# A residual layer with a conditioned linear part, in fp32: the order of the loads, the place of the bias, and the last group by rows

## The reference

```python
hidden = concat([cond, cond], axis=-1)                      # (4, 512)
x_mean = mean(x, axis=1, keepdims=True)
fused = concat([x, x_mean * ones, hidden[:, None] * ones], axis=-1)   # (4, 1024, 1536)
out = x + relu(einsum('bld,do->blo', fused, W) + b)
```

## Time and profile before

| | |
|---|---|
| median of 3 runs | 119.73 us (119.43 to 119.76) |
| profiled execution, first to last instruction | span 117.4 us |
| profiled execution, its own time | not listed apart from the three runs |
| TensorE busy | 103.1 us, 88% of the span |
| VectorE / ACT / POOL busy | 87.0 / 48.2 / 46.7 us |
| moved by DMA | 20.28 MB, mean 173 GB/s |

### The profile page before, as it was taken

How to read it: one execution, slowest core, us unless ns; L and a number is a source line. 1 busy time by engine, 2 the same in 40 slices (tenths; PEclk the granted TensorE clock), 3 DMA queues, 4 the chain that set the end, 5 groups by cost and what they waited for, 6 DMA issues and landing times.

```text
span 117.4 us, 1775 instructions
## 1 busy us (share of the span) xinstructions
PE 103.1 (88%) x490; PEld 82.0 (70%) x490; DVE 87.0 (74%) x163; ACT 48.2 (41%) x118; POOL 46.7 (40%) x46
## 2 busy tenths in 40 slices
PE   5919999935999879997999999999999999999910
PEld 2309998812478568875888888778888886999900
DVE  1028859860289799999999995499999996897640
ACT  4057516700105988006848700077495001833310
POOL 6358310034000000089785840046856339992000
PEclk9995999999599999999999999999999999999995
DMA  2999999999999999990785809400076292295986
GB/s 89 258 228 229 220 212 232 380 240 223 222 224 221 224 220 221 220 167 4 163 197 127 236 12 233 113 0 0 0 170 188 51 248 58 62 241 135 253 219 170
DMA packets 35975, 20.28 MB, mean 173 GB/s; under 512 B 1920, under 2 KB 34688, under 8 KB 35968
## 3 DMA queue, kind: packets, MB, share of 16 engines
q1 hardware_dynamic: 34528, 18.88, 74.5%
q10 hardware_dynamic: 1248, 0.79, 2.5%
q0 software_dynamic: 192, 0.52, 1.8%
HBM read 11.80 MB, written 8.39 MB: 172 GB/s over the span
## 4 chain that ended last, share of the span: by engine, by line
PE 49%; SPq 23%; DMA 10%; DVE 9%; issue 3%; ACT 2%; ACTq 0%
PE ps_y L410 47%; SPq L162 15%; DMA xa<-in_x_dram 10%; SPq L141 3%; DVE back L317 2%; SPq L171 2%; DVE w2x L334 2%; DVE ps_xt L300 2%; PE ps_mean L428 1%; ACT xh L236 1%; DVE xl L306 1%; ACT relu_t L256 1%; DVE bias_row L348 1%; SPq L169 1%; SPq L173 1%
## 5 line engine op out<-in xcount | busy, mean ns | idle before, releaser
L410 PE MATMUL ps_y<-xh,w1h 128*128 128x256 f32 (+2 forms) x160 | 55.1, 370 | 4.3 <-ACT xh L236 2.4
L206 POOL TENSOR_TENSOR xa<-xa,back 128x512 f32 x28 | 36.0, 1304 | 42.8 <-DVE back L317 42.8
L410 PE MATMUL ps_y<-xl,w1h 128*128 128x256 f32 (+2 forms) x160 | 52.3, 353 | 0.0
L410 PE MATMUL ps_y<-xh,w1l 128*128 (+2 forms) x144 | 50.3, 366 | 0.0
L410 PEld LDWEIGHTS ps_y<-xh,w1h 128*128 128x128 f32 x160 | 29.5, 197 | 11.0 <-issue 4.4
L256 ACT ACTIVATE relu_t<-ps_y,bias 128x512 f32<-128x512 f32 (+1 forms) x32 | 19.9, 633 | 33.0 <-DVE bias L351 25.6
L410 PEld LDWEIGHTS ps_y<-xl,w1h 128*128 128x128 f32 x160 | 29.5, 196 | 4.8 <-issue 1.2
L300 DVE STREAM_TRANSPOSE ps_xt<-xa 128x512 f32<-128x512 f32 (+1 forms) x36 | 22.2, 641 | 13.5 <-DMA xa<-in_x_dram 13.2
L236 ACT ACTIVATE xh<-ps_xt 128x512 fp32r<-128x512 f32 (+1 forms) x36 | 19.7, 549 | 26.2 <-DVE ps_xt L300 25.9
L410 PEld LDWEIGHTS ps_y<-xh,w1l 128*128 128x128 f32 x144 | 27.1, 189 | 4.5
L306 DVE TENSOR_TENSOR xl<-ps_xt,xh 128x512 fp32r<-128x512 f32 (+1 forms) x36 | 22.2, 618 | 4.2 <-ACT xh L236 4.2
(11 more groups left out here) (21 smaller groups left out, 22.1 us busy)
## 6 DMA issues: line engine op xcount, KB each, us to landing
xa<-in_x_dram SPq DMA_DIRECT2D x28, 256.0 KB, 6.5
out_dram<-xa SPq DMA_DIRECT2D x28, 256.0 KB, 3.8
xa<-in_x_dram SPq DMA_DIRECT2D x8, 128.0 KB, 5.9
w<-in_L_cond_W_dram SPq DMA_DIRECT2D x4, 256.0 KB, 6.8
w<-in_L_cond_W_dram SPq DMA_DIRECT2D x2, 512.0 KB, 9.7
w<-in_L_cond_W_dram POOLq DMA_DIRECT2D x4, 128.0 KB, 4.7
out_dram<-xa SPq DMA_DIRECT2D x4, 128.0 KB, 2.7
out_dram<-xa ACTq DMA_DIRECT2D x4, 128.0 KB, 2.4
```

The costliest lines, as they stand in the source:

```text
L206: nc.gpsimd.tensor_tensor(rows, rows, back[:, t], ALU.add).then_inc(added, 1)
L410: return nc.tensor.matmul(ps_y[:, t, ls], lhs, rhs, start=start, stop=stop, skip_group_check=True)
```

## The change

W1 is loaded by blocks k of 128 features (four DMAs of 64 KB each), behind x0's first half, which comes on two queues. W1's block 0 is rounded half on VectorE and half on ACT; block 1 on ACT in two halves that PE takes as pairs of tiles. PE does group 0's low-W1 products between the others and takes the first two tiles of group 1 block by block. All eight tiles of batch 0 and two of group 2 are set aside by ACT (`save`; two of them in `w1`'s place). W3, its halves not summed, is multiplied inside group 2's second tile, 16 instructions of 128 columns to four quadrants; the mean products are four such instructions each. The last group is computed by rows (x stationary, W1 moving), its bias comes as a line through DRAM, x is read again by rows, and it is stored by rows. Two adds of group 6 move from POOL to VectorE. Warm-up products are 12.

```diff
-WARM = 14
+WARM = 12
+    DVE_ADDS = 2
+    SAVED = H * NK + 2
+    bias_line = nc.dram_tensor("bias_line", [D], F32).ap()
...
 sync:
-            load_x0(sp, 0)
-            load_w1(sp, 1, range(0, 2), w1_landed)
-            load_x0(sp, 1)
-            load_x(1, 1)
...
+            load_x0(sp, 0, LOW)
+            load_w1(sp, 0, 1, LOW)
+            load_w1(sp, 1, 2, LOW)
+            load_w1(sp, 2, 3, LOW)
+            load_w1(sp, 3, 4, LOW)
+            load_x0(sp, 1, ORDER)
+            load_x(sp, 1, ORDER)
+            load_x(sp, 2, ORDER)
+            load_w2(sp, ORDER)
+            load_x(sp, 3, ORDER)
             for r in range(2):
                 sp.dma_start(w3[:, r], w3v[r]).then_inc(w3_landed, 16)
+            for g in range(SLOTS, G):
+                load_x(sp, g, ORDER)
+            sp.wait_ge(const_summed, 1)
+            for r in range(NR):
+                sp.dma_start(last_x[:, r], x_rows[LAST, :, r]).then_inc(last_x_landed, 16)
+            for g in range(LAST):
+                if g == LAST - 2:
+                    sp.wait_ge(bias_summed, B)
+                    for j in range(NQ):
+                        sp.dma_start(bias_line[P * j:P * j + P], bias_row[Q * j + B - 1]).then_inc(bias_stored, 16)
+                    sp.wait_ge(bias_stored, 16 * NQ)
+                    sp.dma_start(last_bias[:], bias_line.partition_broadcast(P)).then_inc(last_bias_landed, 16)
...
 gpsimd:
+            pool.wait_ge(x0_landed[0], 16 * NQ)
+            for j in HIGH:
+                pool.dma_start(w1[Q * j:Q * j + Q, NK - 1:NK], wv[0, j, :, NK - 1:NK]).then_inc(w1_rest_landed, 16)
...
-            nc.gpsimd.tensor_tensor(w3sum[:], w3[:, 0], w3[:, 1], ALU.add).then_inc(w3_added, 1)
...
 scalar:
+            load_x0(act, 0, HIGH)
             act.wait_ge(ones_set, 1)
             nc.scalar.activation(act_warm[:], ones[:, 0:1], ACT.Relu)
+            load_w1(act, 0, 1, HIGH)
+            load_w1(act, 1, 2, HIGH)
+            load_w1(act, 2, 3, HIGH)
...
             x_high(0)
+            w1_high(0, DVE_T, NK)
             x_high(1)
+            w1_high(1, 0, NK // 2)
+            w1_high(1, NK // 2, NK)
             for k in range(2, NK):
+                x_high(k)
                 w1_high(k)
...
 vector:
             turn_x(0)
+            turn_x(1)
+            dve.wait_ge(w1_landed[0], 16 * NQ)
+            nc.vector.tensor_copy(as_tiles(w1h[:, 0])[:, 0:DVE_T], by_tile(w1[:, 0])[:, 0:DVE_T]).then_inc(w1h_first_ready, 1)
+            x_low(0)
...
+            def last_rows(step, r, y, cols):
+                biased = relu_t[:, NK + r, cols]
+                dve.wait_ge(y_ready, NK * LAST + step)
+                nc.vector.tensor_tensor(biased, y, last_bias[:, cols], ALU.add).then_inc(last_biased, 1)
+                dve.wait_ge(last_biased, step)
+                nc.vector.scalar_tensor_tensor(out=last_x[:, r, cols], in0=biased, scalar=0.0, in1=last_x[:, r, cols],
+                                               op0=ALU.max, op1=ALU.add).then_inc(last_added, 1)
...
 tensor:
-                nc.tensor.matmul(ps_mean[:], ones[:], w2x[:], start=True, stop=True).then_inc(mean_done, 1)
+                for j in range(NQ):
+                    last = nc.tensor.matmul(ps_mean[Q * j:Q * j + Q, 0:P], ones[:, 0:Q], w2x[:, P * j:P * j + P], start=True, stop=True)
+                last.then_inc(mean_done, 1)
...
+            def const_product():
+                pe.wait_ge(cond_spread, 1)
+                pe.wait_ge(w3_landed, 16 * 2)
+                for r in range(2):
+                    for k in range(CK):
+                        for j in range(NQ):
+                            last = nc.tensor.matmul(ps_const[Q * j:Q * j + Q, 0:P], cond_t[:, k], w3[:, r, k, P * j:P * j + P],
+                                                    start=(r == 0 and k == 0), stop=(r == 1 and k == CK - 1))
+                last.then_inc(const_summed, 1)
...
+            def last_product(y, k, r, cols_h, cols_l, start, stop):
+                rows = slice(P * r, P * r + P)
+                slot = LAST % SLOTS
+                nc.tensor.matmul(y, xh[:, slot, k, rows], cols_h, start=start, stop=False, skip_group_check=True)
+                nc.tensor.matmul(y, xh[:, slot, k, rows], cols_l, start=False, stop=False, skip_group_check=True)
+                return nc.tensor.matmul(y, xl[:, slot, k, rows], cols_h, start=False, stop=stop, skip_group_check=True)
```

More of the change, by code:

```diff
@@ L28 @@
 ORDER = (0, 2, 1, 3)
+LOW, HIGH = (0, 1), (2, 3)
 NL = 512
@@ L148, in store_last, with load_x @@
[L148 to L154, removed]
+        def load_x(eng, g, quadrants):
+            for l in range(0, LB, LB // H):
+                for j in quadrants:
+                    eng.dma_start(xa[Q * j:Q * j + Q, g, l:l + LB // H], xv[g, j, :, l:l + LB // H]).then_inc(x_landed[g], 16)
@@ new lines, in load_w1, with load_w2, place @@
+        def load_w1(eng, first, end, quadrants):
+            for j in quadrants:
+                eng.dma_start(w1[Q * j:Q * j + Q, first:end], wv[0, j, :, first:end]).then_inc(w1_landed[first], 16)
+        def load_w2(eng, quadrants):
+            for j in quadrants:
+                eng.dma_start(w2[Q * j:Q * j + Q], wv[1, j]).then_inc(w2_landed, 16)
+        last_x = w3[:].rearrange("p r k o -> p (r k) o")
+        def place(n):
+            return w1[:, n - RELU_RING] if RELU_RING <= n < SAVED else relu_t[:, n % RELU_RING]
@@ new lines, in _ @@
+            save(0)
+            save(1)
+            x_high(pieces_to(H) - 2)
+            x_high(pieces_to(H) - 1)
+            save(2)
+            save(3)
+            n_x = pieces_to(H)
+            x_high(n_x)
+            x_high(n_x + 1)
+            save(NK)
+            x_high(n_x + 2)
+            x_high(n_x + 3)
+            save(NK + 1)
+            save(NK + 2)
+            n_x += NK
+            x_high(n_x)
+            x_high(n_x + 1)
+            save(NK + 3)
+            x_high(n_x + 2)
@@ L369, in _ @@
             turn_x(n_x)
-            turn_and_split(n_x, n_x + 1)
+            turn_and_split(n_x, n_x + NK)
             dve.wait_ge(const_summed, 1)
-            dve.wait_ge(b_landed, 16)
-            for j in range(NQ):
-                rows, cols = slice(Q * j, Q * j + Q), slice(P * j, P * j + P)
-                nc.vector.tensor_tensor(const_row[rows], ps_const[rows, cols], b_row[rows, cols], ALU.add).then_inc(const_ready, 1)
-            dve.wait_ge(const_ready, NQ)
+            dve.wait_ge(b_landed, 16 * NQ)
@@ L442, in _ @@
                         mm(t, ls, w1h[:, k, t], xl[:, 0, k, ls])
+                    if half == 0 and k > 0:
+                        group0_low(half, k - 1)
+                    elif half == 1:
+                        group0_low(half, k)
+                if half == 0:
+                    group0_low(half, NK - 1)
+            for k in range(NK):
+                pe.wait_ge(xl_ready, pieces_to(1) + k + 1)
+                for t in (0, 1):
+                    if k == 0:
+                        pe.wait_ge(y_saved, t + 1)
+                    last = product(1, k, t)
+                    if k == NK - 1:
+                        last.then_inc(y_ready, 1)
@@ new lines, in _ @@
+                    last = product(H % SLOTS, k, t)
+                last.then_inc(y_ready, 1)
+            pe.wait_ge(bias_ready, 1)
+            mean_bias(1)
+            for g in range(H + 1, LAST):
+                for t in range(NK):
+                    if NK * (g - 1) + t < SAVED:
+                        pe.wait_ge(y_saved, NK * (g - 1) + t + 1)
+                    else:
+                        pe.wait_ge(relu_done, NK * (g - 1) + t + 1)
+                    tile(g, g % SLOTS, t)
+                    if g % H == 0 and g < LAST - 1 and t == 2:
+                        pe.wait_ge(bias_ready, g // H)
+                        mean_bias(g // H)
```

362 lines of the change are left out of this document (211 added, 151 removed).

## The result

The changed kernel takes **102.55 us** (median of 6 runs, 102.35 to 102.92), beside 119.75 for the kernel before on the same chip: a ratio of 0.859, 95% interval 0.855 to 0.863. The direction was forecast; the size was not: 110.0 us, with a range that ended at 107.5. The profiled execution took 102.84, its span is 101.0. Some executions of these kernels are slower as a whole, at a lower granted clock; the ratios and their intervals leave them out, the medians do not.

What follows compares the result with a forecast made beforehand. TensorE, busy 103.1 of 117.4 us, was taken to set the end; 6.9 + 12.1 + 27.5 + 45.4 + 11.2 + 4.6 = 107.7, plus 2.3 from span to run median, gave 110.0 us, range 107.5 to 113.8.

Steps and rivals of the forecast that it cites:

- Start: Before the first real product: x0's first half issued earlier on two queues, PE starts at 6.9, 1.9 us sooner.
- The full clock: At the start: 1.1 us idle after warm-up leaves the granted clock at 1.00, where 2.4 us idle had left 0.50.
- Group 0: First group: 96 narrow products, 11.5 us, plus 0.6 for the first block's gaps: 12.1, ending at 19.0 instead of 21.6.
- Groups 1 and 2: Middle of the kernel: 27.5 us replace 32.9, with PE's waits for W3 and relu gone.
- I take 3.8 and 0.96: Groups 1 and 2: W3's small products cost 3.8 us, a mean product 0.96, each record priced as a narrow product, 0.12.
- The lower bound of the prediction: Small W3 and mean products: if the four quadrants overlap, they cost 1.0 and 0.24 us.
- The rival's own price: Small products overlap: PE saves 3.4 by group 3, relu(10) 1.1 and w2x 0.7 late, 1.6 remain: 108.4; chance 0.17.
- the count of 4.7 us per MB: Load landings in groups 1 and 2, counted from 2.5 on: x1, the third MB, lands at 16.6.
- cold start and VectorE together: Two rivals: clock not held in first blocks, 111.7, chance 0.20; VectorE becomes the bound, 112.4, chance 0.17.
- Groups 3 to 6 and the last group: PE's later work: 45.4 us to 91.9 if VectorE keeps up, then 11.2 instead of 11.6, to 103.1.
- Tail: After PE's end: 4.6 us instead of 5.4, with stores behind SP's wait for the bias draining to about 107.
- The rival on the slow side: Last group's bias round trip through DRAM: both transfers take 11.6, landing at 111.5, time 123.4; chance 0.05.

## Why the prediction was right in direction and wrong in size

**What bounds the kernel**: right. 16.4 us of span came off, 6.2 of it from TensorE's busy time and the rest from the time when it was idle, before, between and behind its products.

**Start** (6.9, measured 6.4): right in mechanism. The step "W1's block 0 of the upper quadrants is issued by ACT only after its table load and first activation" was wrong: issues run beside the table load from 1.77. That brings block 0 at 5.97 and not at 6.4; the 0.5 in all is no more than profiles of one kernel can differ by. The full clock came true, but in part by luck: the 1.1 us of idle time that it was to survive did not come, since the twelve warm-up products started each 0.43 us to the end and joined the first product.

**Group 0** (12.1, measured 11.8) held.

**Groups 1 and 2**: here the forecast failed, at the step "I take 3.8 and 0.96". The upper bound was taken because a 256-column product was the nearest row. The W3 products and the first mean product were to cost 4.8 and cost 1.6, each other mean product 0.96 and cost 0.56: with the two of groups 3 to 6, 7.7 us against 3.3, 4.4 of the 7.2 between sum and profile. It was mis-sized twice over: in turn a record costs 0.026 from start to start, in one quadrant 0.071, my price was 0.12. The lower bound of the prediction, 1.0 and 0.24, is near for W3 (1.08 by the record); for a mean product it is under half of what it costs, because it has nothing for the change between wide and small products. I had the lower bound as a rival with 0.17.

**The rival's own price failed too.** It said that of 3.4 us saved only 1.6 would remain, as relu(10) and w2x would be late: 108.4. By its own bounds the saving is 2.8 + 2 x 0.72 = 4.3 by group 3 and 5.7 with the two mean products that follow, which it left out: 104.3 with nothing taken back, a time that my range did not reach. And nothing was taken back. VectorE was through with x3's last piece at 35.9, where the forecast had 38.4, and the bias was there at 36.8, where it had 40.4. The step behind it is the count of 4.7 us per MB "at 222 GB/s": the loads ran at 247, and 0.9 us of it is from the DMAs of half the size, which I had costed at nothing and never thought a gain. VectorE 1.0 us later costs nothing, 2.3 later 0.8. (The upper end of the range, 113.8, is a slip: cold start and VectorE together, 1.7 and 2.4 on 110.0, are 114.1.)

**Groups 3 to 6 and the last group**: 45.4 against 44.9, 11.2 against 11.1; VectorE kept up, w2x was ready 1.0 and 1.9 us early, and two mean products at 0.56 instead of 0.96 are 0.8, more than the difference.

**Tail** (4.6, measured 2.8): the step that failed is the landing of the bias. Its trip, with four issues, took 5.4 us (83.2 to 88.6), where the forecast had 7.7 (88.3 to 96), and it began 5.1 us earlier while row 0 was wanted 4.4 earlier: from 1.4 late to 1.6 early. So the stores left at 86.8, not 92.8, and didn't drain behind PE. The rival on the slow side is real as a mechanism (a landing 5.0 later costs 4.2), and by that price, an estimate, a landing some 20 us later would be needed to tie with the kernel before.

## What to carry to other kernels

Where no row shows an operation, and its two bounds are 4 us apart on the engine that sets the end, neither bound is a forecast: carry both through the whole sum, and work out the follow-up costs (who is late next) again for each, with every stage's times moved along. A product that writes only 32 partitions is best issued to the four quadrants in turn (0.026 us against 0.071 here), in one stretch, since each change between wide and small products costs 0.2 here. Read costs from start to start; the chain's durations had a mean product at 0.36 where it costs 0.56. A wait that is taken away in one place is worth little until the chain behind it (here x2's landing, bias, relu) comes earlier as well: look for the next instruction that the same late transfer holds up, or free the buffer without it, as `save` does.

## What the runs showed of the hardware that I had not expected

- fp32 products with 32 output partitions and 128 columns (two records each) start a record each 0.026 us when consecutive instructions go to different quadrants, each 0.071 when to the same. The first starts 0.32 us or more behind a wide product, where another wide one starts 0.227 behind it.
- Loads of x in 128 KB DMAs ran at a mean of 247 GB/s, in 256 KB ones at 231, over the same six slices of one profile each; other kernels with the 128 KB ones had 239 to 262 from 7.5 to 22.5 us.
- ACT's queue issued three DMAs from 1.77 to 3.12 while ACT loaded a table (1.70 to 2.98).
- After 2.23 us idle the products ran at half pace for 3.5 us (two narrow ones in 0.43 us, as at the granted clock of 0.50 in the kernel before), although the window of that stretch gives a granted clock of 1.00. That the clock was low there is a reading of the pace; the column doesn't show it:

```profile
6.00:9.60 3.60, 3.44 (x16) 3.47 (x17) 2.43 (x7) 2.77 (x11) 3.43 (x4) 1.00 0.89 251
```

- One store of 128 KB in four issues ended 1.2 us later than in one.
